# A four-layer residual stack: the LSTM's new cell is written to PSUM for the tanh and copied to SBUF later

## The chip, the core and the metric

The kernel runs on one core of a Trainium2 chip. The metric is the device time of one launch in microseconds (us), the median over several executions. "ns" is used where a microsecond is too coarse. TensorE is PE in the profile's rows, its weight loads are PEld, VectorE is DVE, ScalarE is ACT, GpSimd is POOL and the queue that issues most of the DMAs is SP.

## What is computed

Four sequences of 1024 tokens with 512 features pass through four residual layers. Layer 0 is a plain RNN, layer 1 a small state-space scan, layer 2 an LSTM, and layer 3 a product with a matrix of its own for each sequence. The core of the reference, with `x` (4, 1024, 512):

```
def rnn_step(prev_h, xw_t):                      # layer 0, xW = x @ Wx + b
    next_h = tanh(xw_t + prev_h @ Wh)
def ssm_step(state, (u_t, b_t, c_t)):            # layer 1, 64 states
    state = decay * state + dt * b_t * u_t
    y_t = c_t * state
def lstm_step((prev_h, prev_c), xw_t):           # layer 2, xW = x @ Wx + b
    A = xw_t + prev_h @ Wh                       # 4 gates of 512
    i, f, o, g = sigmoid(A0), sigmoid(A1), sigmoid(A2), tanh(A3)
    next_c = f * prev_c + i * g
    next_h = o * tanh(next_c)
x = x + rnn(x); x = x + ssm(x); x = x + lstm(x)
x = x + (x + x @ layer[n])                       # layer 3
```

The recurrences of layers 0 and 2 are 1024 steps long each, and a step needs the one before.

## The kernel before

**Tiling.** Time is cut into 32 chunks of 32 steps (`CT = 32`, `NCH = 32`). The layers work on different chunks at once: while the RNN is at chunk i, the state-space layer ("mid") works on chunk i-1 and the LSTM on chunk i-2, and the output layer on chunk i-3. So an ordinary chunk has 32 rounds, in each of which one LSTM step and one RNN step are made, and the rest of the work is spread over fixed rounds by constants at the top of the file. The programs of chunks 0 to 3 and of the last chunks are written out; chunks 4 to 29 run in a hardware loop, two chunks to an iteration, so every second change of chunk is a jump back on each engine. There are 30 chunks in which the RNN, the state-space layer and the LSTM all run.

**An LSTM step.** The 512 hidden units are split in two halves, h = 0 and h = 1. PE multiplies the hidden state, held as a high and a low f16 part (`lstm_h_parts`), with the f16 parts of Wh into the banks `ps_lstm0` and `ps_lstm1` (L1027, 64 matmuls). It waits for `lstm_h_ready0` ahead of the first 24 of them and for `lstm_h_ready1` ahead of the 25th; with the 40th the first half's sums are complete. DVE transposes the sums of a half into SBUF (L745), adds hi part, lo part and input into spare columns of `ps_lstm0` (`reduce`, L750), and ACT takes one tanh over the gates there (L487; sigmoids are had from tanh by scaling). DVE forms the two products i*g and f*c (L756) and the new cell (`new_cell`, L761), ACT takes the tanh of the cell (`tanh_cell`, L496), DVE multiplies it with the output gate for the f32 hidden state (L778) and for its f16 hi part (L781), and subtracts for the lo part (L785), which frees PE for the next step. The row of the cell lies in the same SBUF tile as the gates (`lstm_gates_2c`), because L756 reads g and the old cell as one operand.

**The RNN step** is woven into the same round: PE L1066 into `ps_rnn`, DVE transposes (L854) and adds (L859, into spare columns of `ps_rnn`), ACT tanh (L510), DVE hi part (L898) and lo part (L900).

**The order on DVE** is the order in which the program writes it, quoted for the part that matters:

```
p_at = products(1, s)
tanh_done(0, s)
h_part(0, s)
next_x_filled(0, s)
at = hi_part(0)
new_cell(1, p_at)
lo_part(0, s, at)
if w["mid"]:
    ssm_stage(s, 0)
tanh_done(1, s)
```

`ssm_stage` is the state-space layer's DVE work. It has a part 0 (here) and a part 2 (between the LSTM's last lo part and the RNN's hi part), both in rounds 3 to 8 of a chunk only. After the RNN's lo part (L900) the round is over, and the next instruction of DVE is the next round's transpose. At the end of a chunk, `next_chunk` waits for `go_vec`, clears it, and the loop jumps. GpSimd fills the inputs for later rounds (L351, L365) and adds a piece of the residual every four rounds (L370, L377).

## Time and profile before

| | |
|---|---|
| median of 3 runs | 3904.15 us (3904.12 to 3905.38) |
| the profiled execution's own time | 3902.77 us |
| its span, first to last instruction | 3900.9 us |
| PE / PEld busy | 3624.2 / 3057.5 us |
| DVE busy | 3258.3 us, 19155 instructions |
| ACT busy | 1648.3 us |
| POOL busy | 775.4 us |
| mean granted TensorE clock | 0.997 |

The profiled execution took 1.4 us less than the median. Its span leaves out 1.9 us of its time. Instructions on DVE overlap at their ends in the profile (the next one starts before the last one's write has been acknowledged), so the distance from start to start is what an instruction costs its engine, and its duration plus a hand-over is what it costs the one that waits for its result.

### The profile page before, as it was taken

How to read it: one execution, taken by the hardware profiler on the slowest of the kernel's cores; microseconds unless marked ns; L12 is line 12 of the kernel's file. 1: busy time of each engine (PE TensorE's matmuls, PEld its weight loads, DVE VectorE, ACT ScalarE, POOL GpSimd, SP SyncE). 2: the span in 40 equal slices, each digit the busy share in tenths (PEclk: the TensorE clock that was granted, in tenths of full speed). 3: DMA queues.
4: the chain of work that ended last, by engine and by line, in shares of the span. 5: the costliest groups of instructions: out<-in, count | busy, mean ns of one | idle time of the engine just before them, and what ended most of it. 6: DMA issues, size and time to landing. Idle time of an engine off the chain costs nothing.

```text
span 3900.9 us, 255334 instructions
## 1 busy us (share of the span) xinstructions
PE 3624.2 (93%) x110596; PEld 3057.5 (78%) x110596; DVE 3258.3 (84%) x19155; ACT 1648.3 (42%) x8244; POOL 775.4 (20%) x3623
## 2 busy tenths in 40 slices
PE   7899999999999999999999999999999999999875
PEld 5688788888888888888888888888888888877754
DVE  6688888888888888888888888888888888888766
ACT  4244444444444444444444444444444444444332
POOL 0122122222222222222222222222222222212111
PEclk9999999999999999999999999999999999999999
DMA  7100000000000000000000000000000000000000
GB/s 277 49 7 7 10 10 10 8 9 7 10 10 10 10 7 7 10 10 10 10 7 7 10 10 10 10 8 9 7 10 10 9 10 7 7 7 7 7 6 8
DMA packets 19109, 63.32 MB, mean 16 GB/s; under 512 B 3958, under 2 KB 4526, under 8 KB 14914
## 3 DMA queue, kind: packets, MB, share of 16 engines
q1 hardware_dynamic: 17692, 46.67, 3.7%
q8 instruction: 868, 14.22, 1.5%
q14 instruction: 255, 2.09, 0.2%
q10 hardware_dynamic: 294, 0.33, 0.0%
HBM read 38.48 MB, written 8.39 MB: 12 GB/s over the span
## 4 chain that ended last, share of the span: by engine, by line
DVE 53%; PE 41%; issue 4%; DMA 1%; ACT 1%; SPq 0%; ACTq 0%; DVEq 0%; POOL 0%; POOLq 0%
PE ps_lstm L1027 33%; DVE lstm_sums L745 19%; DVE ps_lstm L750 8%; DVE lstm_ig_fc L756 6%; DVE rnn_sums L854 5%; DVE lstm_gates_2c L761 5%; DVE lstm_h_parts L785 3%; PE ps_rnn L1066 2%; DVE lstm_h_scaled L778 2%; DVE lstm_h_parts L781 2%; PE ps_lstm_in_b L1108 2%; PE ps_ssm L1108 1%; PE ps_lstm_in_a L1171 1%; DMA layer_plus_2I<-in_L_cond_w 1%; DVE rnn_h_parts L900 1%
## 5 line engine op out<-in xcount | busy, mean ns | idle before, releaser
L1027 PE MATMUL ps_lstm<-lstm_Wh_parts,lstm_h_parts 128*20 128x256 f16 x65472 | 1974.7, 273 | 236.3 <-DVE lstm_h_parts L785 156.7
L1027 PEld LDWEIGHTS ps_lstm<-lstm_Wh_parts,lstm_h_parts 128*20 128x20 f16 x65472 | 1546.5, 91 | 639.7 <-DVE lstm_h_parts L785 484.9
L745 DVE STREAM_TRANSPOSE lstm_sums<-ps_lstm 128x256 f32<-128x256 f32 x2048 | 912.8, 446 | 206.6 <-PE ps_lstm L1027 178.1
L487 ACT ACTIVATE lstm_gates_2c<-ps_lstm 128x32 f32<-128x32 f32 x2048 | 403.8, 197 | 1421.2 <-DVE ps_lstm L750 1421.2
L351 POOL COPY lstm_sums<-lstm_in 128x32 f32<-128x32 f32 x2048 | 424.2, 210 | 1749.1 <-DVE ps_lstm L750 1749.1
L1066 PE MATMUL ps_rnn<-rnn_Wh_parts,rnn_h_parts 128*20 128x128 f16 x32736 | 637.1, 220 | 22.8 <-DVE rnn_h_parts L900 20.9
L1066 PEld LDWEIGHTS ps_rnn<-rnn_Wh_parts,rnn_h_parts 128*20 128x20 f16 x32736 | 548.3, 92 | 55.2 <-DVE rnn_h_parts L900 37.6
L750 DVE TENSOR_REDUCE ps_lstm<-lstm_sums 128x32 f32<-128x96 f32 x2048 | 555.0, 271 | 35.2
L496 ACT ACTIVATE lstm_tanh_c<-lstm_gates_2c 128x8 f32<-128x8 f32 x2048 | 419.2, 205 | 254.4 <-DVE lstm_gates_2c L761 254.4
L781 DVE TENSOR_TENSOR lstm_h_parts<-lstm_o_scaled,lstm_tanh_c 128x8 f16<-128x8 f32 x2048 | 334.3, 163 | 129.3 <-ACT lstm_tanh_c L496 45.2
L492 ACT ACTIVATE lstm_o_scaled<-lstm_gates_2c 128x8 f32<-128x8 f32 x2048 | 427.4, 209 | 32.1
L510 ACT ACTIVATE rnn_h<-ps_rnn 128x16 f32<-128x16 f32 x1024 | 187.6, 183 | 519.4 <-DVE ps_rnn L859 519.4
L756 DVE SCALAR_TENSOR_TENSOR lstm_ig_fc<-lstm_gates_2c 128x16 f32<-128x16 f32 x2048 | 351.6, 172 | 12.7 <-ACT lstm_gates_2c L487 12.7
L898 DVE TENSOR_SCALAR rnn_h_parts<-rnn_h 128x16 f16<-128x16 f32 x1024 | 223.2, 218 | 155.3 <-ACT rnn_h L510 154.3
L854 DVE STREAM_TRANSPOSE rnn_sums<-ps_rnn 128x128 f32<-128x128 f32 x1024 | 317.3, 310 | 40.5 <-PE ps_rnn L1066 38.3
L785 DVE TENSOR_TENSOR lstm_h_parts<-lstm_h_scaled,lstm_h_parts 128x8 f16<-128x8 f32 x2048 | 341.6, 167 | 2.2
L778 DVE TENSOR_TENSOR lstm_h_scaled<-lstm_o_scaled,lstm_tanh_c 128x8 f32<-128x8 f32 x2048 | 335.1, 164 | 0.0
L761 DVE SCALAR_TENSOR_TENSOR lstm_gates_2c<-lstm_ig_fc 128x8 f32<-128x8 f32 x2048 | 323.6, 158 | 2.2 <-issue 2.2
L1154 PE MATMUL ps_lstm_in_b<-x,lstm_Wx 128*128 128x128 f32 x2048 | 296.5, 288 | 0.0
L1154 PE MATMUL ps_lstm_in_a<-x,lstm_Wx 128*128 128x128 f32 x2048 | 296.5, 288 | 0.0
L1154 PEld LDWEIGHTS ps_lstm_in_a<-x,lstm_Wx 128*128 128x128 f32 x2048 | 247.8, 191 | 34.1 <-issue 7.8
L1154 PEld LDWEIGHTS ps_lstm_in_b<-x,lstm_Wx 128*128 128x128 f32 x2048 | 247.8, 191 | 28.9 <-issue 1.7
(186 smaller groups left out, 2662.7 us busy)
## 6 DMA issues: line engine op xcount, KB each, us to landing
layer_plus_2I<-in_L_cond_w SPq DMA_DIRECT2D x16, 1024.0 KB, 6.6
out<-out_rows SPq DMA_DIRECT2D x128, 64.0 KB, 1.6
x_rows<-in_x SPq DMA_DIRECT2D x31, 256.0 KB
lstm_Wx<-in_L_cond_Wh SPq DMA_DIRECT2D x1, 4096.0 KB, 17.8
lstm_Wx<-in_L_cond_Wx SPq DMA_DIRECT2D x1, 4096.0 KB, 13.6
layer_plus_2I<-in_L_cond_Wh SPq DMA_DIRECT2D x1, 1024.0 KB, 8.5
rnn_Wx<-in_L_cond_Wx SPq DMA_DIRECT2D x1, 1024.0 KB, 10.9
lstm_in<-in_L_cond_w SPq DMA_DIRECT2D x1, 1024.0 KB, 9.9
```

The source lines that it names most:

```text
L351: Q.tensor_copy(tr[h][s % 2][:, :, XS:XS + NB], xl[par][:, s, h * HG:(h + 1) * HG, :]).then_inc(S[f"lstm_in_ready{h}"], 1)
L492: A.activation(o_s[h][:, :], gate[h][:, 2, :], ACT.Copy, scale=H_SCALE, bias=H_SCALE)
L496: A.activation(tc[h][:, :], cell[h], ACT.Tanh, scale=0.5).then_inc(S[f"lstm_tanhc{h}"], 1)
L745: return mark(V.transpose(tr[h][s % 2][:, :, 0:QC], psL[h][:, 0:HW].rearrange("p (g c) -> p g c", c=QC)))
L750: V.tensor_reduce(arg[h], three.rearrange("p g s n -> p g n s"), AX.X, ALU.add).then_inc(S[f"lstm_summed{h}"], 1)
L756: return mark(V.scalar_tensor_tensor(out=prod[h][:, :, :], in0=gate[h][:, 0:2, :], scalar=1.0, in1=gate[h][:, G - 1:G + 1, :], op0=ALU.add ...
L761: V.scalar_tensor_tensor(out=cell[h], in0=prod[h][:, 1, :], scalar=0.5, in1=prod[h][:, 0, :], op0=ALU.mult, op1=ALU.add).then_inc(S[f"lstm ...
L785: V.tensor_tensor(half(hls, h)[:, :, LO:LO + NB], half(hl, h)[:, :, s, :], half(hls, h)[:, :, 0:NB], ALU.subtract).then_inc(S[f"lstm_h_rea ...
L854: return mark(V.transpose(tr_r[s % 2][:, :, 0:QC], psR[:, 0:RW].rearrange("p (g c) -> p g c", c=QC)))
L1027: ins = mm(psL[h][QC * j:QC * j + LO + NB, 0:HW], hls[:, k, :], whl[:, k, h, e, j, :], start=(k == 0 and e == 0), stop=(k == KB - 1 and e ...
L1066: last = mm(psR[QC * j:QC * j + LO + NB, 0:RW], hrs[:, k, :], whr[:, k, e, j, :], start=(k == 0 and e == 0), stop=(k == KB - 1 and e == 1) ...
L1154: last = mm(psI[b % 2][:, TOK * b:TOK * (b + 1)], w_, x2[:, k, :, :].rearrange("p t n -> p (t n)"), start=(k == 0), stop=(k == KB - 1))
```

## The change

The new cell goes to eight spare columns of PSUM: the first half's to `ps_lstm1` behind the LSTM's sums, the second half's to `ps_rnn` behind the RNN's sums and arguments. ACT's tanh reads it there. The copy in SBUF, which the next step's products read, is made by repeating the same operation with SBUF as the target (`keep_cell`), for both halves, at the end of DVE's round. Nothing waits for these two but the end of the chunk: there DVE waits for the second of them (`kept_at`) before it goes on to the next chunk. Their products (`lstm_ig_fc`) stay unwritten until the next round, so the repeated operation has its inputs.

```
+        cell_p = [psL1[:, HW:HW + HB * NB], psR[:, RW + KB * NB:RW + KB * NB + HB * NB]]
...
                 def tanh_cell(h, s):
                     act.wait_ge(S[f"lstm_cell{h}"], s + 1)
-                    A.activation(tc[h][:, :], cell[h], ACT.Tanh, scale=0.5).then_inc(S[f"lstm_tanhc{h}"], 1)
+                    A.activation(tc[h][:, :], cell_p[h], ACT.Tanh, scale=0.5).then_inc(S[f"lstm_tanhc{h}"], 1)
...
                 def new_cell(h, at):
                     vec.wait_ge(S["vec_done"], at)
-                    V.scalar_tensor_tensor(out=cell[h], in0=prod[h][:, 1, :], scalar=0.5, in1=prod[h][:, 0, :],
+                    V.scalar_tensor_tensor(out=cell_p[h], in0=prod[h][:, 1, :], scalar=0.5, in1=prod[h][:, 0, :],
                                            op0=ALU.mult, op1=ALU.add).then_inc(S[f"lstm_cell{h}"], 1)
+
+                def keep_cell(h):
+                    return mark(V.scalar_tensor_tensor(out=cell[h], in0=prod[h][:, 1, :], scalar=0.5, in1=prod[h][:, 0, :],
+                                                       op0=ALU.mult, op1=ALU.add))
...
                                                op0=ALU.mult, op1=ALU.subtract).then_inc(S["rnn_h_ready"], 1)
+                    if w["lstm"]:
+                        keep_cell(0)
+                        kept_at = keep_cell(1)
                     if known in (0, 1):
                         prepare(CT * known + s)
+                if w["lstm"]:
+                    vec.wait_ge(S["vec_done"], kept_at)
                 next_chunk(vec, "vec")
```

On DVE, in any ordinary round inside the loop, the second part of the round reads as follows before the change, from the first half's hidden state to the next round's transpose (`_1` in a semaphore's name is the set of the odd chunks):

```order
L778 TENSOR_TENSOR lstm_h_scaled<-lstm_o_scaled,lstm_tanh_c 128x2x4 [waits lstm_tanhc0_1]
L781 TENSOR_TENSOR lstm_h_parts<-lstm_o_scaled,lstm_tanh_c 128x2x4 [waits lstm_in_ready0_1]
L761 SCALAR_TENSOR_TENSOR lstm_gates_2c<-lstm_ig_fc 128x8 [waits vec_done_1]
L785 TENSOR_TENSOR lstm_h_parts<-lstm_h_scaled,lstm_h_parts 128x2x4 [waits vec_done_1]
L781 TENSOR_TENSOR lstm_h_parts<-lstm_o_scaled,lstm_tanh_c 128x2x4 [waits lstm_tanhc1_1]
L778 TENSOR_TENSOR lstm_h_scaled<-lstm_o_scaled,lstm_tanh_c 128x2x4 [waits lstm_in_ready1_1]
L859 TENSOR_REDUCE ps_rnn<-rnn_sums 128x16 [waits vec_done_1]
L785 TENSOR_TENSOR lstm_h_parts<-lstm_h_scaled,lstm_h_parts 128x2x4 [waits vec_done_1]
L898 TENSOR_SCALAR rnn_h_parts<-rnn_h 128x4x4 [waits rnn_tanh_1]
L900 SCALAR_TENSOR_TENSOR rnn_h_parts<-rnn_h,rnn_h_parts 128x4x4 [waits vec_done_1]
L745 STREAM_TRANSPOSE lstm_sums<-ps_lstm 128x8x32 [waits lstm_mm0_1]
```

The same stretch of DVE's program after the change (lines are numbered up to five higher):

```order
L783 TENSOR_TENSOR lstm_h_scaled<-lstm_o_scaled,lstm_tanh_c 128x2x4 [waits lstm_tanhc0_1]
L786 TENSOR_TENSOR lstm_h_parts<-lstm_o_scaled,lstm_tanh_c 128x2x4 [waits lstm_in_ready0_1]
L762 SCALAR_TENSOR_TENSOR ps_rnn<-lstm_ig_fc 128x8 [waits vec_done_1]
L790 TENSOR_TENSOR lstm_h_parts<-lstm_h_scaled,lstm_h_parts 128x2x4 [waits vec_done_1]
L786 TENSOR_TENSOR lstm_h_parts<-lstm_o_scaled,lstm_tanh_c 128x2x4 [waits lstm_tanhc1_1]
L783 TENSOR_TENSOR lstm_h_scaled<-lstm_o_scaled,lstm_tanh_c 128x2x4 [waits lstm_in_ready1_1]
L864 TENSOR_REDUCE ps_rnn<-rnn_sums 128x16 [waits vec_done_1]
L790 TENSOR_TENSOR lstm_h_parts<-lstm_h_scaled,lstm_h_parts 128x2x4 [waits vec_done_1]
L903 TENSOR_SCALAR rnn_h_parts<-rnn_h 128x4x4 [waits rnn_tanh_1]
L905 SCALAR_TENSOR_TENSOR rnn_h_parts<-rnn_h,rnn_h_parts 128x4x4 [waits vec_done_1]
L766 SCALAR_TENSOR_TENSOR lstm_gates_2c<-lstm_ig_fc 128x8 x2
L746 STREAM_TRANSPOSE lstm_sums<-ps_lstm 128x8x32 [waits lstm_mm0_1]
```

The new cell stays in its place and only its target is another (`ps_rnn` for the second half, `ps_lstm` for the first, a few rows earlier). Two instructions, which wait for nothing, are added between the RNN's lo part and the transpose.

On DVE at the end of a loop iteration, ahead of the jump back, there stands before the change:

```order
L898 TENSOR_SCALAR rnn_h_parts<-rnn_h 128x4x4 [waits rnn_tanh_1]
L900 SCALAR_TENSOR_TENSOR rnn_h_parts<-rnn_h,rnn_h_parts 128x4x4 [waits vec_done_1]
L255 ISA [waits go_vec]
L246 REGISTER_ALU
L246 COMPARE_AND_BRANCH
```

And after it:

```order
L903 TENSOR_SCALAR rnn_h_parts<-rnn_h 128x4x4 [waits rnn_tanh_1]
L905 SCALAR_TENSOR_TENSOR rnn_h_parts<-rnn_h,rnn_h_parts 128x4x4 [waits vec_done_1]
L766 SCALAR_TENSOR_TENSOR lstm_gates_2c<-lstm_ig_fc 128x8 x2
L256 ISA [waits go_vec,vec_done_1]
L247 REGISTER_ALU
L247 COMPARE_AND_BRANCH
```

The clearing of the semaphore (the ISA row), and with it the jump behind it, now also waits for `vec_done`, that is until the second kept cell has been written. Before, it waited for `go_vec` alone and did not wait for the RNN's lo part.

On ACT, the two tanh of a round read another tile and nothing moves. Before:

```order
L487 ACTIVATE lstm_gates_2c<-ps_lstm 128x32 [waits lstm_summed1_0]
L496 ACTIVATE lstm_tanh_c<-lstm_gates_2c 128x8 [waits lstm_cell0_0]
L492 ACTIVATE lstm_o_scaled<-lstm_gates_2c 128x8 [waits lstm_gated1_0]
L496 ACTIVATE lstm_tanh_c<-lstm_gates_2c 128x8 [waits lstm_cell1_0]
L510 ACTIVATE rnn_h<-ps_rnn 128x4x4 [waits rnn_summed_0]
```

After:

```order
L488 ACTIVATE lstm_gates_2c<-ps_lstm 128x32 [waits lstm_summed1_0]
L497 ACTIVATE lstm_tanh_c<-ps_lstm 128x8 [waits lstm_cell0_0]
L493 ACTIVATE lstm_o_scaled<-lstm_gates_2c 128x8 [waits lstm_gated1_0]
L497 ACTIVATE lstm_tanh_c<-ps_rnn 128x8 [waits lstm_cell1_0]
L511 ACTIVATE rnn_h<-ps_rnn 128x4x4 [waits rnn_summed_0]
```

The waits are the same; the tanh of either half now has a PSUM bank as its source.

## Rows read from the trace of the kernel before

**Rows 1.** The page: the chain that ended last, shares of the span by engine.

```profile
DVE 53%; PE 41%; issue 4%; DMA 1%; ACT 1%; SPq 0%; ACTq 0%; DVEq 0%; POOL 0%; POOLq 0%
```

**Rows 2.** Timeline of one ordinary round: start, duration, engine, line, [idle before].

```profile
2001.15 0.45 DVE L745 STREAM_TRANSPOSE lstm_sums<-ps_lstm 128x256 f32<-128x256 f32 x1 [0.23 <-PE ps_lstm L1027]
...
2002.69 0.20 ACT L496 ACTIVATE lstm_tanh_c<-lstm_gates_2c 128x8 f32<-128x8 f32 x1
...
2002.83 0.18 DVE L756 SCALAR_TENSOR_TENSOR lstm_ig_fc<-lstm_gates_2c 128x16 f32<-128x16 f32 x1
2002.92 0.17 DVE L778 TENSOR_TENSOR lstm_h_scaled<-lstm_o_scaled,lstm_tanh_c 128x8 f32<-128x8 f32 x1
2003.01 0.16 DVE L781 TENSOR_TENSOR lstm_h_parts<-lstm_o_scaled,lstm_tanh_c 128x8 f16<-128x8 f32 x1
2003.09 0.16 DVE L761 SCALAR_TENSOR_TENSOR lstm_gates_2c<-lstm_ig_fc 128x8 f32<-128x8 f32 x1
...
2003.28 0.21 ACT L496 ACTIVATE lstm_tanh_c<-lstm_gates_2c 128x8 f32<-128x8 f32 x1 [0.24 <-DVE lstm_gates_2c L761]
...
2003.52 0.17 DVE L781 TENSOR_TENSOR lstm_h_parts<-lstm_o_scaled,lstm_tanh_c 128x8 f16<-128x8 f32 x1 [0.15 <-ACT lstm_tanh_c L496]
...
2003.80 0.16 DVE L785 TENSOR_TENSOR lstm_h_parts<-lstm_h_scaled,lstm_h_parts 128x8 f16<-128x8 f32 x1
...
2004.35 0.18 DVE L900 SCALAR_TENSOR_TENSOR rnn_h_parts<-rnn_h,rnn_h_parts 128x16 f16<-128x16 f32 x1
2004.75 0.45 DVE L745 STREAM_TRANSPOSE lstm_sums<-ps_lstm 128x256 f32<-128x256 f32 x1 [0.22 <-PE ps_lstm L1027]
```

**Rows 3.** Timeline of PE's weight loads in the same round, two narrow windows.

```profile
2003.42 0.55 PEld L1027 LDWEIGHTS ps_lstm<-lstm_Wh_parts,lstm_h_parts 128*20 128x20 f16 x24 [0.33 <-DVE lstm_h_parts L785]
...
2004.02 0.28 PEld L1027 LDWEIGHTS ps_lstm<-lstm_Wh_parts,lstm_h_parts 128*20 128x20 f16 x12
```

**Rows 4.** Groups by line, ACT: shapes, count, busy us, mean ns of one.

```profile
L496 ACT ACTIVATE lstm_tanh_c<-lstm_gates_2c 128x8 f32<-128x8 f32 x2048 | 419.2, 205 | 254.4 <-DVE lstm_gates_2c L761 254.4
L487 ACT ACTIVATE lstm_gates_2c<-ps_lstm 128x32 f32<-128x32 f32 x2048 | 403.8, 197 | 1421.2 <-DVE ps_lstm L750 1421.2
L510 ACT ACTIVATE rnn_h<-ps_rnn 128x16 f32<-128x16 f32 x1024 | 187.6, 183 | 519.4 <-DVE ps_rnn L859 519.4
```

**Rows 5.** Groups by line, DVE: writes into SBUF and into PSUM.

```profile
L601 DVE MEMSET ps_lstm<- 128x512 f32 x2 | 1.0, 485 | 0.2
L601 DVE MEMSET x1T<- 128x560 f32 x1 | 0.5, 525 | 0.1
L601 DVE MEMSET aeT<- 128x128 f32 x1 | 0.2, 165 | 0.0
...
L750 DVE TENSOR_REDUCE ps_lstm<-lstm_sums 128x32 f32<-128x96 f32 x2048 | 555.0, 271 | 35.2
L859 DVE TENSOR_REDUCE ps_rnn<-rnn_sums 128x16 f32<-128x48 f32 x1024 | 214.5, 210 | 2.2
```

**Rows 6.** DVE timeline at the ends of rounds 4 and 7 of one chunk.

```profile
1936.13 0.18 DVE L900 SCALAR_TENSOR_TENSOR rnn_h_parts<-rnn_h,rnn_h_parts 128x16 f16<-128x16 f32 x1
1936.23 0.45 DVE L745 STREAM_TRANSPOSE lstm_sums<-ps_lstm 128x256 f32<-128x256 f32 x1
...
1946.87 0.18 DVE L900 SCALAR_TENSOR_TENSOR rnn_h_parts<-rnn_h,rnn_h_parts 128x16 f16<-128x16 f32 x1
1947.06 0.45 DVE L745 STREAM_TRANSPOSE lstm_sums<-ps_lstm 128x256 f32<-128x256 f32 x1
```

**Rows 7.** DVE timeline at the end of a round with a GpSimd piece.

```profile
2008.09 0.17 DVE L900 SCALAR_TENSOR_TENSOR rnn_h_parts<-rnn_h,rnn_h_parts 128x16 f16<-128x16 f32 x1
2008.35 0.45 DVE L745 STREAM_TRANSPOSE lstm_sums<-ps_lstm 128x256 f32<-128x256 f32 x1
```

**Rows 8.** Timeline at a jump back of the loop: PE's products, DVE's first transpose.

```profile
1569.21 1.93 PE L1027 MATMUL ps_lstm<-lstm_Wh_parts,lstm_h_parts 128*20 128x256 f16 x64 [0.36 <-DVE lstm_h_parts L785]
...
1571.00 0.45 DVE L745 STREAM_TRANSPOSE lstm_sums<-ps_lstm 128x256 f32<-128x256 f32 x1 [0.68 <-PE ps_lstm L1027]
```

## The prediction

> **What bounds the kernel now.** I read the page first. No engine is full, and the chain that ended last changes hands between DVE (53%) and PE (41%), with ACT at 1% [rows 1]. That is a recurrence: the LSTM step goes round PE, DVE, ACT and DVE, 1024 times. So I read one ordinary round in the timeline, from its first transpose (2001.15) to the next round's (2004.75): 3.60 us [rows 2]. The 32 chunks x 32 rounds of this length are 3686 us of the 3901, and the other rounds differ little. What the change is worth must be read from which of the round's waits end last.
>
> The round's second part runs like this [rows 2]. ACT starts the first half's cell tanh at 2002.69 and ends it at 2002.89 (0.20). DVE starts L756 of the second half at 2002.83 and L778 of the first at 2002.92, the moment the tanh is there plus a hand-over of 0.03. Then L781 (2003.01) and the second half's new cell, L761 (2003.09), follow at 0.09 and 0.08. That cell is complete at 2003.25, ACT starts its tanh at 2003.28 and ends at 2003.49, and DVE, which has sat idle for 0.15 with "ACT lstm_tanh_c" named as releaser, goes on at 2003.52. From there its instructions follow each other down to the second lo part, 2003.80 to 2003.96. PE loads 24 weights from 2003.42, the last of them over at 2003.97, and its 25th starts at 2004.02, 0.06 behind the end of the lo part [rows 3]. 24 loads took 0.55, some 0.02 apart from start to start, so the 25th was wanted about 0.1 before it came. So **the second half's tanh is on the path**: new cell, tanh, hi part, lo part, PE's 25th product, next transpose. The first half reaches the path too, since L761 of the second half stands behind its L778 and L781.
>
> **What the change does to that path.** Three terms.
>
> *The tanh's source.* The cell's tanh takes 205 ns on average from SBUF with 8 elements. From PSUM ACT takes 183 ns for 16 and 197 ns for 32 elements [rows 4]: 0.9 ns an element, which makes 176 ns for 8. The saving is 29 ns, and for the second half, which the timeline shows at 0.21 against 0.20 for the first, 30. Its bounds: 22 ns (205 less the 183 of the 16 elements, no slope) and 34 (0.21 us less 176). It counts in full, since DVE idles for this tanh alone. For the first half it counts only as far as DVE can start L778 sooner: L756 of 16 elements stands 0.09 ahead of it, and L900, also 16 elements, holds the next instruction off for 0.10 where nothing else does [rows 2, 6]. That leaves 0 to 0.01 us; I take 4 ns.
>
> *The cell's target.* No row shows L761's operation writing PSUM. The nearest rows [rows 5]: memsets into SBUF took 165 ns for 128 and 525 ns for 560 elements, 0.83 ns an element over 58, which makes 485 for 512 elements, and into PSUM 512 elements took 485. By this the target costs nothing. The reductions that write PSUM took 271 ns for 96 elements and 210 for 48: 1.27 an element over a fixed 149, or, if an element costs 1.05 ns, midway between the memsets' slope and this one, 160 to 170 fixed. L761 into SBUF took 0.16 for 8 elements [rows 2], some 150 fixed. So the second bound is +20 ns, and an outer one is +50: L761 would then last the 210 of the shorter reduction, elements and all. I take +4, near the memsets, since the steeper line fits both reductions. The first half's cell has cover: its tanh starts behind ACT's own gates tanh, so its write may end later at no cost.
>
> A rule speaks against this. The Trainium skill, Perfetto Trace Analysis, section Optimizing Scalar/DVE Operations, gives a data-access overhead of about 60 ns for DVE on SBUF and about 125 on PSUM, and about 93 and 51 ns for ScalarE. ScalarE's 42 ns would be more than the 30 of the rows. DVE's 65 ns more, if a write pays it, would turn the sum of the terms from +30 into about -19 ns a round. The memset rows do not show such a price; they are no scalar_tensor_tensor, so it stays a rival below.
>
> So a round is shorter by 30 + 4 - 4 = **30 ns**, x 1024 = **30.7 us**. PE can follow: its 25th product moves 30 ns nearer, inside the 100 that it had waited.
>
> *The two kept cells.* They are one more piece of 8 elements each. Start to start such an instruction costs DVE 0.08 (L781 to L761 [rows 2]), by the finer readings 0.075, and L900 costs 0.09. So the transpose can start no sooner than 0.24 behind L900's start. Ordinary rounds give it 0.40 [rows 2], so they are hidden, with 0.16 to spare. Nine rounds of a chunk have a GpSimd piece that makes the RNN's hi part late; there L900 and the transpose are 0.26 apart [rows 7]. Both move forward by the 30 ns, so the cover there is 0.26 - 0.24 = 0.02: hidden, but barely. In the state-space rounds it isn't hidden. In round 4 the transpose comes 0.10 behind L900, in round 7 0.19 [rows 6]; rounds 5 and 8 read as round 4. Cost: 0.14 x 3 + 0.05 = 0.47 us a chunk, x 30 chunks = **14.1 us**. Two small effects I let cancel, each under 1 us: in round 4 a state-space instruction already fills DVE's wait for the tanh, so that round's 30 ns are lost, and the rounds behind a late transpose find PE and ACT readier than before.
>
> *The end of a chunk.* DVE's jump used to be prepared while L900 ran. Now it waits until the second kept cell is written: 0.09 + 0.08 + 0.16 + 0.03 = 0.36 behind L900's start, against next to nothing. Behind a jump back the first transpose had 0.68 of idle ahead of it against 0.22 in an ordinary round [rows 2, 8]. PE is named as releaser, but it had begun the step's products 1.79 ahead of the transpose, against 1.33 in an ordinary round [rows 3, 8]. So it is DVE's own jump that is late, and the 0.35 come in full: 12 jumps back (13 iterations), 4.2 us. Inside an iteration there is no jump and the spare time takes most of it: 0.06 x 18 = 1.1 us; into and out of the loop 0.7. Together **6.0 us**. Nothing else waits for the kept cells: ACT, PE and GpSimd get their signals from other instructions, and no DMA queue is passed.
>
> **Sum.** -30.7 + 14.1 + 6.0 = -10.6 us. Against the profiled execution's 3902.8 that is 3892.2. The median of the runs stands 1.4 above it, so **3893.5 us** is predicted, 0.27% faster.
>
> **Rivals.** What this kernel's measurement can tell from no change is about 0.2%, 7.8 us: 3896.3 to 3912.0.
>
> 1. *As forecast*, with a gain of 27 to 40 ns a round: 20.1 us of costs less 27.6 to 41 us, 3883 to 3896. Chance 0.50.
> 2. *The costs eat the gain.* PSUM writes cost 7 to 20 ns more (the reductions' bound), so 14 to 27 ns are left of a round: 3896 to 3910. For it: the reductions at 1.04 ns. Against: the memsets. Chance 0.28.
> 3. *The tanh is not faster for its source.* 183 and 197 ns were shapes of other instructions, and nothing is saved: costs alone, 3924. For it: no row has 8 elements from PSUM. Against: 32 elements from PSUM take less than 8 from SBUF. Chance 0.08.
> 4. *Slower: a PSUM write by this operation is dear.* At the outer bound of 50 ns a round is 16 ns longer: 16.4 + 20.1 = 36.5, so 3941. From 15 ns on the change breaks even, and from 22 on it is slower by over 0.2%. The place is L762 into `ps_rnn`, whose end ACT waits for. For it: DVE's shortest row into PSUM is 210 ns [rows 5]. Against: the memsets. Chance 0.08. The Trainium skill's Perfetto Trace Analysis (Optimizing Scalar/DVE Operations) is on this side; its 65 ns with the 30 of the tanh would make it 3956, an estimate by that page.
> 5. *DVE becomes the bound in the GpSimd rounds.* The cover is 0.02. If a kept cell costs 0.10 start to start and not 0.075, then the nine rounds and the four lose 0.05 less 0.02 or 0.05 each: 0.47 x 30 = 14 us more, 3908. Chance 0.06.
>
> **How the numbers follow.** Rival 1 is the likeliest, and 3893.5 stands inside it, at the sum. Faster by over 0.2%: 0.50. Within: 0.28 + 0.05 = 0.33. Slower: 0.08 + 0.08 + 0.01 = 0.17. The range reaches from the best case of the bounds, 34 + 10 ns and a free write (44 ns, 45 us less 20: 3879, cut to 3882, since three best bounds seldom meet), over cases 1, 2 and 5 to 3910. Cases 3 and 4 stay out, with 0.16, and a little below 3882. The forecast's own range is 3883 to 3896.
>
> **What would show it.** In the changed profile L497 should stand near 176 ns and L762 between 158 and 165. An ordinary round should last 3.57 us. L778's successor L783 should stand 0.09 behind L757, and DVE's wait for the second tanh should shrink from 0.15 to 0.12. L766 should come right behind L905, with the next transpose 0.24 behind L905's start in rounds 4, 5, 7 and 8, and 0.26 in the GpSimd rounds. Behind a jump back the transpose should have 0.88 of idle ahead of it and not 0.68, and stand some 2.15 behind the start of PE's products. The prediction falls if L762 reads 180 ns or more, if ordinary rounds stay at 3.60, or if the GpSimd rounds come out longer than the ordinary ones. The jump's price is the least sure of the costs, because the profile shows only the idle time ahead of the transpose.

## The result: slower by 0.2%, and the profile after

| | before | after |
|---|---|---|
| median of 17 runs each | 3904.61 us | 3912.69 us |
| lowest to highest | 3901.31 to 3910.84 | 3909.95 to 3919.70 |
| ratio, 95% interval | | 1.002 [1.0013, 1.0026] |
| profiled execution: time, span | 3902.77, 3900.9 | 3917.90, 3916.1 |

The change cost 8 us. The prediction said 3893.5 with a range of 3882 to 3910, so it had the sign wrong and the time lies outside the range. The profiled execution of after is 5 us above its own median: its LSTM began 8 us later than in the profile of before, in a stretch (before the first LSTM step) that the change does not touch. There PE's granted clock drops to half, from 2.4 to 1.2 GHz, for some microseconds at other moments in each execution: from 120 us to the LSTM's start its mean was 0.97 in before and 0.90 in after. So all comparisons of traces below are made from the first LSTM transpose to the last. That stretch took 3710.6 us in the profile of before and 3717.8 in that of after: 7.2 us more, near the 8.1 of the medians.

The chain that ended last has more of DVE and less of PE (before: DVE 53%, PE 41% [rows 1]). In after the page shows:

```profile
DVE 64%; PE 26%; issue 5%; ACT 4%; DMA 1%; DVEq 0%; ACTq 0%; SPq 0%; POOL 0%; POOLq 0%
```

This share doesn't say what sets an ordinary round: e3 below, whose ordinary rounds last as before, shows the same 64% and 26%.

The two tanh and the kept cells, from the groups by line of after (shapes, count, busy us, mean ns of one, idle before):

```profile
L497 ACT ACTIVATE lstm_tanh_c<-ps_rnn 128x8 f32<-128x8 f32 x1024 | 181.4, 177 | 253.0 <-DVE ps_rnn L762 253.0
L497 ACT ACTIVATE lstm_tanh_c<-ps_lstm 128x8 f32<-128x8 f32 x1024 | 176.2, 172 | 0.0
...
L766 DVE SCALAR_TENSOR_TENSOR lstm_gates_2c<-lstm_ig_fc 128x8 f32<-128x8 f32 x2048 | 242.6, 160 | 0.0
```

The tanh takes 172 and 177 ns where it took 205 [rows 4]. One ordinary round of after, for [rows 2], again as a timeline (start, duration, engine, line, [idle before]):

```profile
1401.73 0.45 DVE L746 STREAM_TRANSPOSE lstm_sums<-ps_lstm 128x256 f32<-128x256 f32 x1
...
1403.27 0.17 ACT L497 ACTIVATE lstm_tanh_c<-ps_lstm 128x8 f32<-128x8 f32 x1
...
1403.40 0.18 DVE L757 SCALAR_TENSOR_TENSOR lstm_ig_fc<-lstm_gates_2c 128x16 f32<-128x16 f32 x1
1403.50 0.16 DVE L783 TENSOR_TENSOR lstm_h_scaled<-lstm_o_scaled,lstm_tanh_c 128x8 f32<-128x8 f32 x1
1403.58 0.16 DVE L786 TENSOR_TENSOR lstm_h_parts<-lstm_o_scaled,lstm_tanh_c 128x8 f16<-128x8 f32 x1
1403.65 0.17 DVE L762 SCALAR_TENSOR_TENSOR ps_rnn<-lstm_ig_fc 128x8 f32<-128x8 f32 x1
...
1403.85 0.18 ACT L497 ACTIVATE lstm_tanh_c<-ps_rnn 128x8 f32<-128x8 f32 x1 [0.24 <-DVE ps_rnn L762]
...
1404.34 0.17 DVE L790 TENSOR_TENSOR lstm_h_parts<-lstm_h_scaled,lstm_h_parts 128x8 f16<-128x8 f32 x1
...
1404.92 0.17 DVE L905 SCALAR_TENSOR_TENSOR rnn_h_parts<-rnn_h,rnn_h_parts 128x16 f16<-128x16 f32 x1
1405.01 0.23 DVE L766 SCALAR_TENSOR_TENSOR lstm_gates_2c<-lstm_ig_fc 128x8 f32<-128x8 f32 x2
1405.32 0.45 DVE L746 STREAM_TRANSPOSE lstm_sums<-ps_lstm 128x256 f32<-128x256 f32 x1
```

The reader is to compare two distances. The second half's lo part stands 2.61 behind the round's first transpose, against 2.65 before: it has come forward by 0.04. The next round's transpose stands 3.58 behind it (3582 ns by the start times), against 3.60: it has come forward by no more than half of that. So PE got the second half sooner and did nothing with it.

The costs are seen at the ends of other rounds. Timeline of DVE at the end of round 4 (for [rows 6]) and behind a jump back (for [rows 8]) in after:

```profile
1368.81 0.18 DVE L905 SCALAR_TENSOR_TENSOR rnn_h_parts<-rnn_h,rnn_h_parts 128x16 f16<-128x16 f32 x1
1368.91 0.24 DVE L766 SCALAR_TENSOR_TENSOR lstm_gates_2c<-lstm_ig_fc 128x8 f32<-128x8 f32 x2
1369.06 0.44 DVE L746 STREAM_TRANSPOSE lstm_sums<-ps_lstm 128x256 f32<-128x256 f32 x1
...
1578.54 0.45 DVE L746 STREAM_TRANSPOSE lstm_sums<-ps_lstm 128x256 f32<-128x256 f32 x1
...
1582.96 0.45 DVE L746 STREAM_TRANSPOSE lstm_sums<-ps_lstm 128x256 f32<-128x256 f32 x1 [0.90 <-PE ps_lstm L1037]
```

In round 4 the transpose stands 0.25 behind L905, where it stood 0.10 behind L900. Behind the jump it had 0.90 of idle ahead of it, against 0.68 [rows 8], and the last round lasted 4.42 us against 4.07.

The 1023 distances between first transposes, taken from the start times in a trace, can be added up by round of the chunk. This table is used for all the runs; "ordinary" is the median of the rounds 10 to 30.

| run | LSTM stretch, us | rounds 0-3 | rounds 4-9 | rounds 10-30 | round 31 | ordinary, ns | jump, us |
|---|---|---|---|---|---|---|---|
| before | 3710.6 | 472.3 | 696.5 | 2417.4 | 124.5 | 3596 | 4.06 |
| before, profiled again (e8) | 3713.9 | 478.3 | 696.5 | 2415.7 | 123.4 | 3592 | 4.06 |
| after | 3717.8 | 471.8 | 705.1 | 2411.8 | 129.1 | 3583 | 4.40 |
| e1, second half alone | 3715.5 | 473.0 | 699.5 | 2416.0 | 127.1 | 3592 | 4.34 |
| e2, first half alone | 3704.2 | 468.3 | 699.5 | 2408.2 | 128.2 | 3580 | 4.35 |
| e3, two writes alone | 3736.4 | 479.6 | 710.1 | 2418.0 | 128.6 | 3592 | 4.44 |
| e4, copies earlier | 3710.6 | 471.1 | 704.1 | 2410.4 | 125.0 | 3580 | 4.13 |
| e9, the same but for round 8 | 3709.5 | 475.6 | 699.4 | 2410.2 | 124.3 | 3580 | 4.13 |
| e10, earlier in the last round | 3713.4 | 474.4 | 704.5 | 2410.2 | 124.3 | 3580 | 4.13 |
| e7, second lo part later | 3721.2 | 474.9 | 700.8 | 2421.4 | 124.1 | 3600 | 4.06 |
| e6, first half, copy in the gap | 3704.6 | 474.3 | 695.2 | 2410.9 | 124.2 | 3580 | 4.05 |
| e5, both, copies in the gap | 3699.5 | 473.6 | 694.6 | 2407.6 | 123.7 | 3580 | 4.02 |

The second profile of the unchanged kernel says how it is to be read. Rounds 4 to 9 and the jumps repeat exactly. An ordinary round differs by 4 ns from one profile to the other (3596, 3592), so 4 ns are no effect. In rounds 0 to 3, where PE now and then sits idle with "issue" as the only reason, two profiles of one kernel differ by 6 us.

One cost shows in this table that the prediction had no term for. In after, e3, e4, e9 and e10, round 29 of the first chunk of every loop iteration lasts 3.77 us and not 3.58; in e6 it is round 24, and in before, e1, e2, e5 and e7 no round of the loop body does so in every iteration. DVE sits idle there ahead of the RNN's transpose, with no other engine named. From the timeline of DVE in after:

```profile
1457.15 0.32 DVE L859 STREAM_TRANSPOSE rnn_sums<-ps_rnn 128x128 f32<-128x128 f32 x1 [0.18 <-issue]
```

That is 0.19 us in each of 13 iterations, 2.5 us a launch. What causes it is open. It comes and goes with small changes of DVE's program, and the number of added operations alone doesn't decide, since e5 adds as many a round as after and hasn't got it.

### The profile page after: what moved, and what is told of

It is laid out like the page before. It is cut to its first block, busy times and chain, and to the rows that moved or that the text cites. A ratio compares the mean times of both kernels' runs of the same rounds, so it can differ in the third digit from the quotient of the medians.

```text
span 3916.1 us, 257414 instructions
## 1 busy us (share of the span) xinstructions
PE 3634.0 (93%) x110596; PEld 3083.9 (79%) x110596; DVE 3381.8 (86%) x21203; ACT 1616.2 (41%) x8244; POOL 776.1 (20%) x3623
## 4 chain that ended last, share of the span: by engine, by line
DVE 64%; PE 26%; issue 5%; ACT 4%; DMA 1%; DVEq 0%; ACTq 0%; SPq 0%; POOL 0%; POOLq 0%
PE ps_lstm L1037 20%; DVE lstm_sums L746 19%; DVE ps_lstm L751 8%; DVE lstm_ig_fc L757 6%; DVE rnn_sums L859 5%; DVE lstm_h_parts L786 4%; DVE ps_lstm L762 4%; DVE rnn_h_parts L903 3%; DVE lstm_h_scaled L783 3%; DVE rnn_h_parts L905 2%; DVE ps_rnn L762 2%; DVE lstm_h_parts L790 2%; DVE lstm_gates_2c L766 2%; PE ps_rnn L1076 2%; DVE ps_rnn L864 2%
## 5 line engine op out<-in xcount | busy, mean ns | idle before, releaser
L1037 PEld LDWEIGHTS ps_lstm<-lstm_Wh_parts,lstm_h_parts 128*20 128x20 f16 x65472 | 1567.9, 91 | 623.4 <-DVE lstm_h_parts L790 487.7
L786 DVE TENSOR_TENSOR lstm_h_parts<-lstm_o_scaled,lstm_tanh_c 128x8 f16<-128x8 f32 x2048 | 332.7, 162 | 107.4
L757 DVE SCALAR_TENSOR_TENSOR lstm_ig_fc<-lstm_gates_2c 128x16 f32<-128x16 f32 x2048 | 351.4, 172 | 12.1 <-ACT lstm_gates_2c L488 12.1
L783 DVE TENSOR_TENSOR lstm_h_scaled<-lstm_o_scaled,lstm_tanh_c 128x8 f32<-128x8 f32 x2048 | 326.2, 159 | 2.5 <-issue 2.5
L497 ACT ACTIVATE lstm_tanh_c<-ps_rnn 128x8 f32<-128x8 f32 x1024 | 181.4, 177 | 253.0 <-DVE ps_rnn L762 253.0
L766 DVE SCALAR_TENSOR_TENSOR lstm_gates_2c<-lstm_ig_fc 128x8 f32<-128x8 f32 x2048 | 242.6, 160 | 0.0
```

Source lines behind the costliest of these rows:

```text
L757: return mark(V.scalar_tensor_tensor(out=prod[h][:, :, :], in0=gate[h][:, 0:2, :], scalar=1.0, in1=gate[h][:, G - 1:G + 1, :], op0=ALU.add ...
L783: return mark(V.tensor_tensor(half(hl, h)[:, :, s, :], o3[h], t3[h], ALU.mult))
L786: return mark(V.tensor_tensor(half(hls, h)[:, :, 0:NB], o3[h], t3[h], ALU.mult))
L1037: ins = mm(psL[h][QC * j:QC * j + LO + NB, 0:HW], hls[:, k, :], whl[:, k, h, e, j, :], start=(k == 0 and e == 0), stop=(k == KB - 1 and e ...
```

## The experiments

**Theory A**, made after the result: the round is set by the first half alone. Its lo part starts PE, and PE's first 24 products cover the second half. **Theory B** is the prediction's: the second half's tanh is on the path, and something else gave the time back. Runs e1 and e2 split the change.

**e1: only the second half in PSUM, one copy.**

```
-        cell_p = [psL1[:, HW:HW + HB * NB], psR[:, RW + KB * NB:RW + KB * NB + HB * NB]]
+        cell_p = [cell[0], psR[:, RW + KB * NB:RW + KB * NB + HB * NB]]
...
-                        keep_cell(0)
                         kept_at = keep_cell(1)
```

> Only the second half's new cell goes to PSUM, with one kept copy at the end of the round; the first half is as before. Theory A (the round is set by the first half: its lo part starts PE, PE's first 24 products cover the second half's lo part): the second tanh shortens to 177 ns and its lo part comes some 30 ns sooner, but an ordinary round stays at 3.596 us; the copy costs 0.03 to 0.05 us in rounds 4, 5 and 8 (3 us in all) and 0.26 us at each jump back (3 us), so 3909 to 3912 against 3904.6. Theory B (the prediction's: the second half's tanh is on the path): an ordinary round falls to 3.57 us and the time to about 3885.

Measured: 3911.48 us against 3906.98, ratio 1.0015 [1.0006, 1.0024]. Slower, as theory A has it. One round of e1 in the timeline of DVE and ACT:

```profile
1396.25 0.45 DVE L746 STREAM_TRANSPOSE lstm_sums<-ps_lstm 128x256 f32<-128x256 f32 x1
...
1398.38 0.18 ACT L497 ACTIVATE lstm_tanh_c<-ps_rnn 128x8 f32<-128x8 f32 x1 [0.25 <-DVE ps_rnn L762]
...
1398.87 0.17 DVE L790 TENSOR_TENSOR lstm_h_parts<-lstm_h_scaled,lstm_h_parts 128x8 f16<-128x8 f32 x1
...
1399.84 0.45 DVE L746 STREAM_TRANSPOSE lstm_sums<-ps_lstm 128x256 f32<-128x256 f32 x1
```

The second tanh is short, the lo part stands 2.62 behind the transpose (2.65 before), and the next round comes 3.59 behind it; the median of the ordinary rounds is the same 3592 ns as in the second profile of the unchanged kernel. In an ordinary round all that the prediction had counted on is there and buys nothing.

It does buy something where DVE is busy to the end of the round. In round 4 a state-space operation fills DVE's idle time ahead of the second hi part (L781, in e1 L786), and yet DVE goes on no sooner than the tanh lets it. Timeline of DVE in round 4, first in before and then in e1:

```profile
1355.69 0.14 DVE L781 TENSOR_TENSOR lstm_h_parts<-lstm_o_scaled,lstm_tanh_c 128x8 f16<-128x8 f32 x1
1355.74 0.16 DVE L778 TENSOR_TENSOR lstm_h_scaled<-lstm_o_scaled,lstm_tanh_c 128x8 f32<-128x8 f32 x1
...
1362.42 0.12 DVE L786 TENSOR_TENSOR lstm_h_parts<-lstm_o_scaled,lstm_tanh_c 128x8 f16<-128x8 f32 x1
1362.45 0.16 DVE L783 TENSOR_TENSOR lstm_h_scaled<-lstm_o_scaled,lstm_tanh_c 128x8 f32<-128x8 f32 x1
```

The second of the two begins 2452 ns behind the round's transpose in before, which is where it begins in an ordinary round too, and at 2429 in e1. So here the shorter tanh brings DVE forward by 23 ns.

**e2: only the first half in PSUM, one copy.**

```
-        cell_p = [psL1[:, HW:HW + HB * NB], psR[:, RW + KB * NB:RW + KB * NB + HB * NB]]
+        cell_p = [psL1[:, HW:HW + HB * NB], cell[1]]
...
-                        keep_cell(0)
-                        kept_at = keep_cell(1)
+                        kept_at = keep_cell(0)
```

> Only the first half's new cell goes to PSUM, one kept copy. Theory A: an ordinary round falls from 3.596 to 3.583 us, all that the full change had, 11 us over the launch; one copy costs 4 us in the state-space rounds and 3 us at the jumps: 3900 to 3903, faster than before by 0.1%. Theory B: the round falls by 4 ns at most and the time is 3906 to 3908.

Measured: 3902.30 against 3906.98, ratio 0.9991 [0.9982, 1.0000]. Ordinary rounds last 3580 ns. In ordinary rounds the first half alone has all of the gain of the full change, and theory B is out. It is the length of the rounds that says so; the interval of the ratio reaches 1.

**e7: how much room the second half has.** The kernel before, with one more operation ahead of its second lo part, into a tile that nothing reads:

```
+                        V.scalar_tensor_tensor(out=spare, in0=prod[1][:, 1, :], scalar=0.5, in1=prod[1][:, 0, :],
+                                               op0=ALU.mult, op1=ALU.add)
                         lo_part(1, s, at)
```

> The kernel before with one more operation of 8 elements (into a tile that nothing reads) just ahead of the second half's lo part, which so comes 76 ns later. In the kernel before PE's 25th product starts 109 ns behind its 21st, which is its own pace for a group of four, and 66 ns behind the load that the lo part releases. Theory A: the second half was hidden, but by less than 10 ns, so an ordinary round grows by 0.065 to 0.075 us and the time by 65 to 80 us, 3970 to 3985. If it had real slack (some 50 ns or more), the round grows by less than 0.03 and the time stays under 3935.

Measured: 3917.65 against 3908.24, ratio 1.0024 [1.0014, 1.0034]. That is far from 3970: my reading that this half had hardly any room was wrong as well. DVE in one round of e7, as a timeline:

```profile
1397.06 0.45 DVE L746 STREAM_TRANSPOSE lstm_sums<-ps_lstm 128x256 f32<-128x256 f32 x1
...
1399.70 0.15 DVE L891 SCALAR_TENSOR_TENSOR cell_spare<-lstm_ig_fc 128x8 f32<-128x8 f32 x1
1399.77 0.16 DVE L786 TENSOR_TENSOR lstm_h_parts<-lstm_h_scaled,lstm_h_parts 128x8 f16<-128x8 f32 x1
...
1400.65 0.45 DVE L746 STREAM_TRANSPOSE lstm_sums<-ps_lstm 128x256 f32<-128x256 f32 x1 [0.21 <-PE ps_lstm L1030]
```

And the weight loads of the same round in the timeline of PEld:

```profile
1399.33 0.55 PEld L1030 LDWEIGHTS ps_lstm<-lstm_Wh_parts,lstm_h_parts 128*20 128x20 f16 x24 [0.33 <-DVE lstm_h_parts L786]
...
1399.99 0.33 PEld L1030 LDWEIGHTS ps_lstm<-lstm_Wh_parts,lstm_h_parts 128*20 128x20 f16 x16
```

The lo part stands 2.71 behind the transpose, 0.07 later than before, and the 25th load comes 0.66 behind the first and not 0.60. Yet the round lasts 3.59 to 3.60. By the matmuls' own start times, the 25th matmul stands 2933 to 2934 ns behind the round's transpose in both kernels, 110 to 112 behind the 21st, which is how every group of four follows the one before. The load ahead of it began at 2867 in the kernel before and at 2932 in e7. **So the loads run ahead of the matmuls, and a gap between two loads is not a gap between two matmuls.** The second half had about 65 ns of room in the kernel before, and e7 has used it up: by the 29th matmul it is 8 ns further behind the first than in before (777 against 769). The 9 us of e7 are these 4 to 8 ns in ordinary rounds, and its state-space rounds (4.3 us more than before), where DVE's time counts.

**e3: the costs alone.** Cell and tanh as before, but the two repeated operations and the wait are there, into tiles that nothing reads:

```
-        cell_p = [psL1[:, HW:HW + HB * NB], psR[:, RW + KB * NB:RW + KB * NB + HB * NB]]
+        cell_p = cell
+        spare = [sb(f"cell_spare{h}", [P, HB * NB])[:, :] for h in range(NH)]
...
-                    return mark(V.scalar_tensor_tensor(out=cell[h], in0=prod[h][:, 1, :], scalar=0.5, in1=prod[h][:, 0, :],
+                    return mark(V.scalar_tensor_tensor(out=spare[h], in0=prod[h][:, 1, :], scalar=0.5, in1=prod[h][:, 0, :],
```

> Cell and tanh as before; the two repeated operations are made at the end of each round all the same, into two SBUF tiles that nothing reads, with the wait at the end of the chunk. So this has the costs alone. Expected by the prediction's terms: 0.14 us in rounds 4, 5 and 8 and 0.06 in round 7, 13 us; 0.34 at 12 jumps and 0.06 at 18 other chunk ends, 5 us; together 3921 to 3924, ordinary rounds unchanged at 3.596. If the costs lie elsewhere (every round a little longer, or the loads of instructions), ordinary rounds are longer too, or the time is above 3926.

Measured: 3929.52 against 3906.98, ratio 1.0061 [1.0047, 1.0075]. Ordinary rounds are unchanged. Rounds 4 to 9 take 13.6 us more than in both profiles of before, where 13 were expected, and the last rounds 4 to 5 us more. That makes 18 to 19 us, as the prediction's terms have it. But the run is 22.5 us above before, over the 16 to 19 that I expected (3921 to 3924 against 3904.6): the pause in round 29 makes 2.5 of it, and the rest isn't assigned, since rounds 0 to 3 differ by as much in two profiles of one kernel.

**e4: the copies moved up**, to where DVE waits for the RNN's tanh.

```
                         lo_part(1, s, at)
+                        keep_cell(0)
+                        kept_at = keep_cell(1)
...
-                    if w["lstm"]:
-                        keep_cell(0)
-                        kept_at = keep_cell(1)
```

> The full change with the two copies moved up, from behind the RNN's lo part to behind the LSTM's second lo part, where DVE sits idle for the RNN's tanh in an ordinary round. Theory A: the wait at the end of the chunk finds them written, so the jumps are back at 4.06 us and 5 us are saved, but the state-space rounds keep their price, since DVE has no idle time there: 3907 to 3909. If the state-space rounds have idle time at this place after all, up to 12 us more are saved: 3896.

Measured: 3911.60 against 3906.98, ratio 1.0014 [1.0005, 1.0023]. Both halves of the expectation hold in part. The jumps last 4.13 us and not 4.40. Rounds 4 and 5 are back at 3.58, though not by idle time, of which DVE has next to none there. What changes is a state-space operation. Timelines of round 4, first in before and then in e4:

```profile
1356.26 0.32 POOL L370 TENSOR_TENSOR x1T<-xT,rnn_h 128x64 f32<-128x64 f32 x1
1356.27 0.38 DVE L802 TENSOR_TENSOR stage<-stage 128x64 f32<-128x64 f32 x1
...
1364.99 0.31 POOL L371 TENSOR_TENSOR x1T<-xT,rnn_h 128x64 f32<-128x64 f32 x1
1365.14 0.25 DVE L807 TENSOR_TENSOR stage<-stage 128x64 f32<-128x64 f32 x1
```

In before it begins 0.01 behind GpSimd's addition and takes 0.38. The copies push it to 0.15 behind, where it takes 0.25, and its shorter time pays for most of them (round 5 is alike, 385 and 253 ns). But round 8 got longer, from 3.72 before and 3.83 after to 4.00. The end of that round in e4, DVE and GpSimd:

```profile
1379.13 0.23 DVE L766 SCALAR_TENSOR_TENSOR lstm_gates_2c<-lstm_ig_fc 128x8 f32<-128x8 f32 x2
1379.21 0.23 POOL L366 COPY rnn_sums<-rnn_in 128x16 f32<-128x16 f32 x1 [1.08 <-DVE ps_rnn L864]
1379.29 0.17 DVE L833 COPY state<-stage 128x2 f32<-128x2 f32 x1
1379.37 0.74 DVE L838 SCALAR_TENSOR_TENSOR stage<-stage,softplus_A_dt 64x64 f32<-64x64 f32 x2
1379.40 0.31 POOL L371 TENSOR_TENSOR x1T<-xT,rnn_h 128x64 f32<-128x64 f32 x1
1380.14 0.18 DVE L905 TENSOR_SCALAR rnn_h_parts<-rnn_h 128x16 f16<-128x16 f32 x1
```

And the same place in the kernel before:

```profile
1370.51 0.59 DVE L833 SCALAR_TENSOR_TENSOR stage<-stage,softplus_A_dt 64x64 f32<-64x64 f32 x2
1370.67 0.32 POOL L370 TENSOR_TENSOR x1T<-xT,rnn_h 128x64 f32<-128x64 f32 x1
```

The first of the two L838 now begins 0.03 ahead of GpSimd's addition, where it used to begin 0.16 ahead of it, and the pair takes 0.74 and not 0.59.

**e9: the same, but in round 8 the copies stay at the end.**

```
                         lo_part(1, s, at)
+                        if s != SERIES_STEP + 5:
+                            keep_cell(0)
+                            kept_at = keep_cell(1)
...
-                    if w["lstm"]:
+                    if w["lstm"] and s == SERIES_STEP + 5:
                         keep_cell(0)
-                        kept_at = keep_cell(1)
+                        keep_cell(1)
```

> As the run with the copies moved up, but in round 8 they stay at the end of the round. There the moved copies had pushed the state-space operation on 64 partitions next to GpSimd's addition, and it took 0.43 us and not 0.27, and the round was 0.27 us longer than before. If that meeting is the cause, round 8 falls from 4.00 to 3.83 us and the others stay, 5 us less: 3906 or less against 3912 for that run (ratio about 1.000 to before). If the round stays at 4.00, the cause is another.

Measured: 3906.35 against 3909.61, ratio 0.9991 [0.9982, 1.0001]; round 8 is back at 3.83 and the rest as in e4. The place of the copies in that one round costs 5 us. That the meeting with GpSimd is the mechanism fits the two durations, and those of rounds 4 and 5 the other way round; it wasn't tried by taking GpSimd's addition away.

**e10: the price of the chunk's end.** The full change, with the copies earlier in the last round of each chunk only:

```
                         lo_part(1, s, at)
+                        if s == CT - 1:
+                            keep_cell(0)
+                            kept_at = keep_cell(1)
...
-                    if w["lstm"]:
+                    if w["lstm"] and s < CT - 1:
                         keep_cell(0)
-                        kept_at = keep_cell(1)
+                        keep_cell(1)
```

> The full change, but in the last round of each chunk alone the two copies stand behind the LSTM's second lo part, so that the wait at the end of the chunk finds them written. All other rounds as changed. If the jump waits for the copies and for nothing else, the jumps fall from 4.405 to 4.06 or 4.13 us and the other chunk ends from 3.725 to 3.65: 4.5 us less than the changed kernel, about 1.001 times before. If they stay at 4.4, the price lies in the longer program.

Measured: 3911.66 against 3909.61, ratio 1.0004 [0.9994, 1.0013]. Jumps at 4.13, other chunk ends at 3.65, round 31 in all 124.3 us against 129.1 in after. So DVE's wait for the copies was worth 4.8 us. A jump is still 0.07 us longer than before, 0.8 us in all; the wait itself is still in the program there, and no run says what these 0.07 are.

**e8: the kernel before, profiled again.**

> The kernel before, unchanged, profiled a second time on another chip. It tells what two profiles of one kernel differ by: ordinary rounds should again be 3.596 us long (or 3.592, as in the run of the two writes alone; then those 4 ns are no effect of a change), the jumps 4.06, and rounds 1 to 3, in which PE now and then waits for its own instructions, anything within some us in all.

Measured: one time, 3909.05 us, beside 3909.61 for the other runs of before on that chip. Ordinary rounds 3592 ns, jumps 4.06. The 4 ns are thus a difference between two profiles, on two chips, and no effect of e1 or e3, and the gain of an ordinary round is 3592 - 3580 or 3596 - 3583, 12 to 13 ns.

**e6 and e5: the copies in a gap.** Behind the round's first transpose DVE waits for the transpose's last write before it may reduce. The copy of the round before can be made there, since the cell is read only later and `lstm_ig_fc` is overwritten only later. Nothing then stands at the end of a round, and nothing is waited for at the end of a chunk. For e5:

```
                         at = transpose(0, s)
+                        if not (known == 2 and s == 0):
+                            keep_cell(0)
+                            keep_cell(1)
                         reduce(0, s, at)
...
-                    if w["lstm"]:
-                        keep_cell(0)
-                        kept_at = keep_cell(1)
...
-                if w["lstm"]:
-                    vec.wait_ge(S["vec_done"], kept_at)
```

e6 is the same with `cell_p` as in e2 and `keep_cell(0)` alone.

> Only the first half's new cell goes to PSUM, and its copy to SBUF is made in the next round between the first transpose and the first reduction, where DVE waits for the transpose's last write: R0 stands 485 ns behind T0, and behind the transpose DVE is free again after about 365 ns (T1 to P0). The copy needs 76, so 441 is before 485. Theory A: ordinary rounds 3.580 us as in the run with the first half alone, the state-space rounds and the jumps as in the kernel before, since nothing stands at the end of a round and nothing is waited for at the end of a chunk: 3887 to 3892, faster by 0.35 to 0.45%. Theory B (the place does not matter, two operations of DVE cost what they cost): 3900 as before.

> Both halves in PSUM, both copies between the first transpose and the first reduction of the next round. The gap holds one copy but not two: 365 + 76 + 76 = 517 against 485, so every round is 0.032 us longer than the 3.583 of the changed kernel: 3.615, 33 us over the launch, less the 18 us that the end of round and chunk had cost: 3924 to 3930. If DVE is free sooner behind the transpose than I read, both fit and it is 3892.

Measured: e6 3897.62 against 3908.24, ratio 0.9975 [0.9965, 0.9985]; e5 3899.25 against 3908.24, ratio 0.9978 [0.9968, 0.9987]. **Both beat the kernel before, by 11 us and 9 us.** e6 gained less than expected, 0.25% where I had said 0.35 to 0.45; its pause in round 24 costs 2.5 us of the difference. For e5 the expectation of a gap too small was wrong, as the timeline of DVE in e5 shows at the start of a round:

```profile
1396.67 0.45 DVE L746 STREAM_TRANSPOSE lstm_sums<-ps_lstm 128x256 f32<-128x256 f32 x1 [0.22 <-PE ps_lstm L1035]
1397.05 0.20 DVE L766 SCALAR_TENSOR_TENSOR lstm_gates_2c<-lstm_ig_fc 128x8 f32<-128x8 f32 x2
1397.16 0.27 DVE L751 TENSOR_REDUCE ps_lstm<-lstm_sums 128x32 f32<-128x96 f32 x1
```

The pair takes 0.20 from end to end, 0.38 behind the transpose's start, and the reduction starts at 0.49, against 0.485 without them. Two copies cost 8 ns at most there, and the round still lasts 3.58.

## Why the prediction was wrong

**The step that failed** is the one in bold: "the second half's tanh is on the path". I had read it from [rows 3], a pause of PE's weight loads that ended 0.06 behind the second lo part, and concluded that PE's 25th product "was wanted about 0.1 before it came". It was the load that was wanted, not the product. The term sized by it, 30 ns a round or 30.7 us, was 12 to 13 ns, or 12.8 us, and that was the first half's. e1 (the second half alone, nothing gained), e2 (the first half alone, all of the gain) and e7 (the 25th load 65 ns later, the product in its place) show it from three sides for the ordinary rounds. DVE's idle of 0.15 for the second tanh was real, and there of no account.

The trace of before already had it. The chain of that same round, in order of time (start, duration, what), goes through the first half's lo part, and neither the second tanh nor the second lo part is on it:

```profile
2003.17 0.08 DVE lstm_gates_2c L761
2003.24 0.14 DVE lstm_h_parts L785
2003.38 0.04 issue
2003.42 1.30 PE ps_lstm L1027 x40
2004.72 0.02 issue
```

**Where the second half did count** was just where the prediction took it as lost. It said that in round 4 a state-space instruction already fills DVE's wait for the tanh, "so that round's 30 ns are lost". But DVE's time sets the end of that round once the copies stand there, and the tanh's part in it is 23 ns (e1). Rounds 4, 5, 7 and 8 last 34 to 37 ns less in after than in e3, which has the same copies, where the first half is worth 12. In round 8 this holds without copies at the end too: 3724 ns in before, 3713 with the first half alone (e6), 3687 with both (e5). These 23 ns more in four rounds of 30 chunks are 2.8 us.

**What the 12 ns are.** The first half's way to its lo part. I had given it 4 ns, for L783 standing 92 to 93 behind L757 and no longer 97. The other 8 are in the next distance: L783 took 168 ns with the next instruction 85 behind when the first tanh read SBUF, and 159 with 77 when it read PSUM, in every run alike. Together they make 12. e2 shows that they are the first half's. That L783 no longer has to wait, and is shorter for it, is a reading of the start times and wasn't tried by itself.

**The signs that were named** nearly all came: the tanh at 172 to 177 ns, L762 at 166 to 168 where at most 165 was named, DVE's wait for the second tanh at 0.13 after 0.15, 0.25 from L905 to the transpose in round 4, 0.90 of idle behind a jump. None of them could tell whether the second half is on the path. Only the ordinary round could, and it came at 3.58 where 3.57 was said and 3.60 was to refute it.

**The tanh's source** was right: 30 ns said, 28 and 31 measured (200 to 172, 208 to 177).

**The cell's target** was nearly right. L762 takes 165 to 168 ns for either half, against 157 to 159 for L761: +9, where I took +4 from bounds of 0 and 20. The rule of the Trainium skill (Perfetto Trace Analysis, section Optimizing Scalar/DVE Operations), 65 ns more for DVE on PSUM, isn't borne out for a write by this operation; its 42 ns less for ScalarE are more than the 28 to 31 of the trace.

**The kept cells.** In rounds 4 to 9 the writes alone cost 13.6 us (e3), against 14.1 said. In the GpSimd rounds they were hidden, as said: but for round 29, all rounds from 10 on last the same in after. That DVE is simply full in the state-space rounds, as the argument had it, was too simple. With the copies in another place rounds 4 and 5 cost nothing, since an operation beside GpSimd's addition gets shorter by as much (e4), and in the gap behind the transpose no round does (e5, e6), but for the pause of e6.

**The end of a chunk** was said to cost 6.0 us. It cost 0.34 us at a jump, where 0.35 was said, and 0.06 at the other ends: 5.2 us, from which these rounds' own gain of 0.4 is already taken off. Without it 4.8 us are the wait for the copies (e10), and 0.8 stay at the jumps.

**The sum again, with what was measured:** -12.8 - 2.8 + 13.6 + 4.8 + 0.8 + 2.5 (the pause in round 29) = +6.1 us by the terms, +7.2 in the traces and +8.1 in the medians; rounds 0 to 3 are too uneven to say where the rest lies. The costs, 21.7 us where 20.1 was said, had been right within 2 us, though 2.5 of them were a pause that no term stood for. The gain, 15.6 us where 30.7 was said, was wrong by 15. By its time the outcome lies just above rival 2, where the costs eat the gain, but not for rival 2's reason: the write to PSUM cost 9 ns. The tanh did get faster, mostly on a half that an ordinary round doesn't wait for.

## What to carry to other kernels

Before a wait is called part of the path, follow it to the instruction that does the work. On PE that is the matmul and not the weight load: if the matmul starts at its usual distance behind the last one, whatever released the load was early enough. The profile's chain through one such round is a quick first test. A delay put in by hand (one small operation ahead of the suspect) measures the room in one run. And a wait that is hidden in the usual round may count in the few rounds with another limit, so the rounds are best added up by kind.

When an operation is split into an urgent one and one that may be late, the late one isn't free at the end of a round, where it delays whatever comes next in the rounds that are full. It belongs into a gap where its engine waits for its own result, here between a transpose and the reduction of it. And a wait at the end of a loop body, for work issued just ahead of it, holds up the jump.

## What the runs showed of the hardware

- A small ScalarE instruction was 28 to 31 ns shorter with its source in PSUM: 172 and 177 ns for 8 elements, against 200 and 208 from SBUF.
- The same scalar_tensor_tensor on 8 elements took 165 to 168 ns into PSUM and 157 to 160 into SBUF.
- The DVE multiplication that reads the first tanh took 168 ns, and the next instruction followed at 85. With the tanh 28 ns shorter it took 159, and the next followed at 77.
- Two small DVE operations behind a transpose of 256 elements started 373 and 419 ns behind the transpose's start, 46 apart instead of 77, and the first of them took 124 ns.
- Where two DVE operations on 64 partitions began beside a GpSimd addition instead of 0.16 us ahead of it, the pair took 0.74 us and not 0.59. One on 128 partitions and 64 elements took 0.38 us when it began 0.01 behind such an addition, and 0.25 when it began 0.15 behind.
- PE's weight load for the 25th matmul began 66 ns ahead of the matmul or 2 ns ahead of it, and the matmul started in the same place.
- DVE paused for 0.18 us in one fixed round of every loop iteration, with no engine named, in six of twelve traces; which round it was, and whether there was one, changed with the program.
